# Joining LayerNorm statistics on GpSimd instead of VectorE, with the stages of the pipeline moved to other slots

## The reference, cut to what matters

```python
def _layernorm(x, axis=-1, eps=1e-05):
    m = jnp.mean(x, axis=axis, keepdims=True)
    v = jnp.var(x, axis=axis, keepdims=True)
    return (x - m) / jnp.sqrt(v + eps)
...
h = _layernorm(x, axis=-1) * (1 + ca) + sa
x = x + ga * attn(h)        # attn normalises h again: xn = layernorm(h) * gamma + beta, then q, k, v, rope
h = _layernorm(x, axis=-1) * (1 + cb) + sb
x = x + gb * ffn(h)
```

## Time and profile before

| | us |
|---|---|
| median of three runs (3055.15 to 3060.04) | 3057.6 |
| the profiled execution | 3057.38 |
| its span, first to last instruction | 3055.6 |
| busy: TensorE / VectorE / ScalarE / GpSimd | 2754.5 / 2146.6 / 1816.3 / 967.6 |

### The profile page before, as it was taken

The page is one execution under the profiler, slowest core; times in us unless marked ns, Lnnn a source line. Parts: engine busy times, 40 slices in busy tenths (PEclk is TensorE's granted clock), DMA queues, the critical chain, the costliest instruction groups (busy, mean ns, idle before and its releaser), DMA issues. The chain is left out here.

```text
span 3055.6 us, 48203 instructions
## 1 busy us (share of the span) xinstructions
PE 2754.5 (90%) x17467; PEld 1341.3 (44%) x17467; DVE 2146.6 (70%) x3164; ACT 1816.3 (59%) x3723; POOL 967.6 (32%) x1294
## 2 busy tenths in 40 slices
PE   2788889499999999999999999999999699948997
PEld 0444455134444444444444444444444277734664
DVE  4999999587777777777777777777777155552221
ACT  1667777157777777777777777777777544411121
POOL 1666665311221121122112112211211176732231
PEclk8899999589999999999999999999999899978998
DMA  3367766915444544544554454355443287752342
GB/s 95 123 221 235 216 219 219 203 40 106 95 90 99 103 90 91 106 92 90 102 102 87 94 106 92 86 105 102 86 96 79 69 284 265 266 172 77 91 116 43
DMA packets 188549, 386.18 MB, mean 126 GB/s; under 512 B 33413, under 2 KB 104485, under 8 KB 175800
## 3 DMA queue, kind: packets, MB, share of 16 engines
q1 hardware_dynamic: 182170, 374.58, 47.9%
q0 software_dynamic: 6144, 8.52, 1.6%
HBM read 240.65 MB, written 144.53 MB: 126 GB/s over the span
## 5 line engine op out<-in xcount | busy, mean ns | idle before, releaser
L927 DVE TENSOR_REDUCE mx<-ps 128x2 f32<-128x1024 f32 (+3 forms) x1216 | 1371.4, 1167 | 397.7 <-PE ps L1015 302.3
L973 ACT ACTIVATE prob<-ps 128x512 f32<-128x512 f32 (+1 forms) x2560 | 1251.3, 561 | 539.9 <-PE ps L1033 530.9
L1008 PE MATMUL ps<-k_rows,q_rows 96*128 96x512 bf16 (+3 forms) x3072 | 911.2, 332 | 41.3 <-DMA k_rows<-k_parts 34.6
L1033 PE MATMUL ps<-q_rows,k_rows 99*128 99x512 bf16 (+3 forms) x3072 | 907.0, 328 | 14.6 <-ACT prob L973 6.1
L866 POOL TENSOR_SCALAR_AFFINE_SELECT prob<-prob 128x512 f32<-128x512 f32 x512 | 318.7, 634 | 1452.6 <-ACT prob L973 1452.6
L1052 PE MATMUL ps<-prob,v_rows 128*32 128x512 f32 (+3 forms) x6144 | 628.3, 496 | 0.0
L1033 PEld LDWEIGHTS ps<-q_rows,k_rows 99*128 99x128 bf16 x3072 | 273.0, 98 | 599.1 <-ACT prob L973 360.1
L1008 PEld LDWEIGHTS ps<-k_rows,q_rows 96*128 96x128 bf16 x3072 | 289.9, 98 | 271.6 <-DVE mx L927 60.6
L1015 PE MATMUL ps<-mask_b,unit_b 128*128 128x128 bf16 (+2 forms) x1408 | 348.7, 248 | 0.0
L671 PE MATMUL ps<-x_t,w_all 128*128 128x512 f32 x512 | 250.9, 636 | 0.0
L1052 PEld LDWEIGHTS ps<-prob,v_rows 128*32 128x32 f32 x6144 | 134.3, 108 | 245.9 <-ACT prob L973 122.9
(11 more groups left out here) (154 smaller groups left out, 2683.9 us busy)
## 6 DMA issues: line engine op xcount, KB each, us to landing
k_rows<-k_parts SPq DMA_DIRECT2D x384, 128.0 KB, 7.4
v_ones<-v_st SPq DMA_DIRECT2D x64, 512.0 KB, 4.3
v_rows<-v_ones SPq DMA_DIRECT2D x64, 512.0 KB, 9.3
att<-o_sb SPq DMA_DIRECT2D x128, 256.0 KB, 2.5
att_b<-att SPq DMA_DIRECT2D x16, 2048.0 KB, 9.9
q_parts<-stage SPq DMA_DIRECT2D x128, 192.0 KB, 3.3
k_parts<-stage SPq DMA_DIRECT2D x128, 192.0 KB, 3.3
q_rows<-q_parts SPq DMA_DIRECT2D x64, 384.0 KB, 4.6
```

Source lines behind the costliest of these rows:

```text
L927: dve.tensor_reduce(dst, src, AX.X, ALU.max).then_inc(a_free, 1)
L973: nc.scalar.activation(prob[:, (g * NPC + i) % RING, h, 0:w], src, ACT.Exp).then_inc(exp_done, 1)
L1008: ins = pe.matmul(ps[:, at, col:col + w], q[0:ROWS, g, h, i * P:(i + 1) * P], k[0:ROWS, g, h, k0:k0 + w], start=(r == 0), stop=True, skip_ ...
L1033: ins = pe.matmul(ps[:, PS_B + bank(g, n), at:at + w], k[0:AUG, g, h, j * P:(j + 1) * P], q[0:AUG, g, h, q0:q0 + w], start=True, stop=True)
```

## The change

GpSimd now joins the halves, for eight tiles at once, with seven small instructions per statistic on 128 x 8 elements (`join`: sum and difference of the two means, sum of the two squared deviations, and a chain of four more; ScalarE's root scales by 1/256 and VectorE only takes the reciprocal), and forms the centring term with one more (`centre`). The steps get new leads: take_x 23 -> 27, join_x on GpSimd 23, root 19 -> 22, invert_x 18 -> 21, centre_x 20, first_norm 17 -> 19, modulate 16 -> 18, take_h 15 -> 17, join_h on GpSimd 9, root of h 7 -> 8, invert_h 6 -> 7, centre_h 6; START goes from -23 to -27. In a GpSimd slot join and centre stand ahead of modulate and low. SyncE's program, the three buffers of `xin`, and the slots of everything from second_norm on stay as they are. `link` makes GpSimd wait for its own last instruction before the next.

```diff
@@ -343,8 +343,10 @@
         h = sb("h", [P, 2, T, D], F32)
         stx = sb("stx", [P, T, 6], F32)
         sth = sb("sth", [P, T, 6], F32)
-        agx = sb("agx", [P, 2, T, 2], F32)
-        agh = sb("agh", [P, 2, T, 2], F32)
+        sums = sb("sums", [P, 2, T], F32)
+        gap = sb("gap", [P, 2, T], F32)
+        spread = sb("spread", [P, 2, T], F32)
+        half_sum = sb("half_sum", [P, 2, T], F32)
         rsh = sb("rsh", [P, 2, T], F32)
         nmh = sb("nmh", [P, 2, T], F32)
         sd = sb("sd", [P, 2, T], F32)
@@ -359,6 +361,7 @@
         mod_in = tuple(sem(f"p1_mod_in{r}") for r in range(RING))
         stx_done, sth_done = sem("p1_stx"), sem("p1_sth")
         agx_done, agh_done = sem("p1_agx"), sem("p1_agh")
+        pool_chain = sem("p1_pool_chain")
         sdx_done, sdh_done = sem("p1_sdx"), sem("p1_sdh")
         rsx_done, rsh_done = sem("p1_rsx"), sem("p1_rsh")
         ones_set = sem("p1_ones_set")
@@ -385,7 +388,7 @@
         def turned(n):
             return ps[:, PS_QK + n % QR * 2:PS_QK + n % QR * 2 + 2, :]
 
-        START = -23
+        START = -27
         END = B * T + 6
 
         def batch_at(s, lead):
@@ -450,18 +453,9 @@
                     ins = dve.bn_stats(stx[:, t, :], xin[:, r, t, :])
                 ins.then_inc(stx_done, 1)
 
-            def join_x(b):
-                dve.wait_ge(stx_done, 4 * b + 4)
-                for t in range(T):
-                    ins = dve.bn_aggr(agx[:, b % 2, t, :], stx[:, t, :])
-                ins.then_inc(agx_done, 1)
-
             def invert_x(b):
                 dve.wait_ge(sdx_done, b + 1)
                 dve.reciprocal(rsx[:, b, :], sd[:, 0, :]).then_inc(rsx_done, 1)
-                dve.wait_ge(rsx_done, b + 1)
-                dve.scalar_tensor_tensor(nmx[:, b, :], agx[:, b % 2, :, 0], -1.0, rsx[:, b, :], ALU.mult, ALU.mult) \
-                   .then_inc(statx, 1)
 
             def take_h(b, t):
                 if t == 0:
@@ -474,19 +468,10 @@
                     dve.wait_ge(h_done, (b - 1) * T + t + 1)
                 dve.bn_stats(sth[:, t, :], h[:, b % 2, t, :]).then_inc(sth_done, 1)
 
-            def join_h(b):
-                dve.wait_ge(sth_done, b * T + T)
-                for t in range(T):
-                    ins = dve.bn_aggr(agh[:, b % 2, t, :], sth[:, t, :])
-                ins.then_inc(agh_done, 1)
-
             def invert_h(b):
-                p = b % 2
                 dve.wait_ge(sdh_done, b + 1)
-                dve.reciprocal(rsh[:, p, :], sd[:, 1, :]).then_inc(rsh_done, 1)
-                dve.wait_ge(rsh_done, b + 1)
-                dve.scalar_tensor_tensor(nmh[:, p, :], agh[:, p, :, 0], -1.0, rsh[:, p, :], ALU.mult, ALU.mult) \
-                   .then_inc(stath, 1)
+                reuse(dve, xn_done, (b - 1) * T)
+                dve.reciprocal(rsh[:, b % 2, :], sd[:, 1, :]).then_inc(rsh_done, 1)
 
             def multiply(n):
 
@@ -523,22 +508,18 @@
                     take_rest(n - 1)
                 if s % 2 == 0 and 0 <= n < B * NP:
                     combine(n)
-                b, k = batch_at(s, 18)
+                b, k = batch_at(s, 21)
                 if b is not None and k == 0:
                     invert_x(b)
-                b, k = batch_at(s, 6)
+                b, k = batch_at(s, 7)
                 if b is not None and k == 0:
                     invert_h(b)
-                b, k = batch_at(s, 15)
+                b, k = batch_at(s, 17)
                 if b is not None:
                     take_h(b, k)
-                    if k == T - 1:
-                        join_h(b)
-                b, k = batch_at(s, 23)
+                b, k = batch_at(s, 27)
                 if b is not None and k < 4:
                     take_x(b, k)
-                    if k == 3:
-                        join_x(b)
 
             dve.memset(eps[:, :], EPS)
             for s in range(START, END):
@@ -546,10 +527,10 @@
 
         @block.scalar
         def _(act):
-            def root(b, which, ag, ready, done):
+            def root(b, which, ready, done):
                 reuse(act, rsh_done if which else rsx_done, b)
                 act.wait_ge(ready, b + 1)
-                nc.scalar.activation(sd[:, which, :], ag[:, b % 2, :, 1], ACT.Sqrt, bias=eps[:, :]).then_inc(done, 1)
+                nc.scalar.activation(sd[:, which, :], spread[:, which, :], ACT.Sqrt, bias=eps[:, :], scale=1.0 / D).then_inc(done, 1)
 
             def first_norm(b, t):
                 if t == 0:
@@ -593,12 +574,12 @@
                 nc.scalar.copy(parts(n, 1), rest[:, n % 2]).then_inc(mid_done, 1)
 
             def slot(s):
-                b, k = batch_at(s, 19)
+                b, k = batch_at(s, 22)
                 if b is not None and k == 0:
-                    root(b, 0, agx, agx_done, sdx_done)
-                b, k = batch_at(s, 7)
+                    root(b, 0, agx_done, sdx_done)
+                b, k = batch_at(s, 8)
                 if b is not None and k == 0:
-                    root(b, 1, agh, agh_done, sdh_done)
+                    root(b, 1, agh_done, sdh_done)
                 for tiles, b in turned_in(s - 1):
                     for t in tiles:
                         copy_x(b, t, tiles[-1])
@@ -611,7 +592,7 @@
                 n = (s - 5) // 2
                 if s % 2 == 1 and 0 <= n < B * NP:
                     middle(n)
-                b, k = batch_at(s, 17)
+                b, k = batch_at(s, 19)
                 if b is not None:
                     first_norm(b, k)
                 for tiles, b in normed_in(s):
@@ -635,12 +616,49 @@
                     pool.wait_ge(h_mul, b * T + t + 1)
                     pool.tensor_tensor(h[:, p, t, :], h[:, p, t, :], mods[:, r, M_SA, :], ALU.add).then_inc(h_done, 1)
 
+            links = [0]
+
+            def link(ins):
+                links[0] += 1
+                ins.then_inc(pool_chain, 1)
+                pool.wait_ge(pool_chain, links[0])
+
+            def join(b, which, st, ready, count, rooted, done):
+
+                pool.wait_ge(ready, count)
+                reuse(pool, rooted, b)
+                pool.tensor_tensor(sums[:, which, :], st[:, :, 1], st[:, :, 4], ALU.add)
+                pool.tensor_tensor(gap[:, which, :], st[:, :, 1], st[:, :, 4], ALU.subtract)
+                link(pool.tensor_tensor(spread[:, which, :], st[:, :, 2], st[:, :, 5], ALU.add))
+                link(pool.tensor_scalar(half_sum[:, which, :], gap[:, which, :], D / 4.0, None, ALU.mult))
+                link(pool.tensor_tensor(gap[:, which, :], gap[:, which, :], half_sum[:, which, :], ALU.mult))
+                link(pool.tensor_scalar(half_sum[:, which, :], sums[:, which, :], -0.5, None, ALU.mult))
+                pool.tensor_tensor(spread[:, which, :], spread[:, which, :], gap[:, which, :], ALU.add).then_inc(done, 1)
+
+            def centre(which, nm, rs):
+                return pool.tensor_tensor(nm, half_sum[:, which, :], rs, ALU.mult)
+
             def low(n):
                 pool.wait_ge(mid_done, n + 1)
                 pool.tensor_tensor(parts(n, 2), rest[:, n % 2], parts(n, 1), ALU.subtract).then_inc(lo_done, 1)
 
             def slot(s):
-                b, k = batch_at(s, 16)
+                b, k = batch_at(s, 23)
+                if b is not None and k == 0:
+                    join(b, 0, stx, stx_done, 4 * b + 4, sdx_done, agx_done)
+                b, k = batch_at(s, 9)
+                if b is not None and k == 0:
+                    join(b, 1, sth, sth_done, b * T + T, sdh_done, agh_done)
+                b, k = batch_at(s, 20)
+                if b is not None and k == 0:
+                    pool.wait_ge(rsx_done, b + 1)
+                    centre(0, nmx[:, b, :], rsx[:, b, :]).then_inc(statx, 1)
+                b, k = batch_at(s, 6)
+                if b is not None and k == 0:
+                    pool.wait_ge(rsh_done, b + 1)
+                    reuse(pool, xn_done, (b - 1) * T)
+                    centre(1, nmh[:, b % 2, :], rsh[:, b % 2, :]).then_inc(stath, 1)
+                b, k = batch_at(s, 18)
                 if b is not None:
                     modulate(b, k)
                 n = (s - 6) // 2
```

## The result

The changed kernel takes 3139.6 us in the median of four runs (3135.95 to 3140.32), against 3056.9 for the kernel before on the same chip: a ratio of 1.0267 (95% interval 1.0249 to 1.0285), so 83 us slower. The profiled execution took 3140.32.

What follows compares the result with a forecast made beforehand. Phase 1 was taken to run at VectorE's pace, 29.2 us per batch, becoming a 37.3 us ring behind a late load: 3057.4 + 10.7 + 81 - 8.3 = 3140.8, 3141 us; range 3108 to 3185.

Steps and rivals of the forecast that it cites:

- the late load: Phase 1: take_x comes four slots earlier, its load does not; VectorE waits eleven times, 9 to 13 us each.
- the ring: Phase 1: VectorE statistics, GpSimd work, SyncE k stores and load landing in sequence set a 37.3 us period, 8.1 longer.
- start: Before the first multiply: GpSimd's three joins and two centrings, 6.9 us, partly hidden by an earlier wait; taken as +5.
- first wait ends: Slot 13, load 5: VectorE's take_x waits until 156.0 us instead of standing at 145.35, +10.7.
- ten periods: Phase 1 from load 5 to load 15: ten times 8.1 us longer, +81.
- from the last wait to the end of phase 1: After slot 93 no load is outstanding, so work removed from VectorE counts in full, -8.3 us.
- first rival: Load of x in phase 1 isn't late, so only VectorE's relief counts: faster, 3002 us; chance 0.05.
- The ends of the range: Phase 1: small instructions at 0.14 us, faster landing and issues give period 36.1, about 3125; at 0.5 us some 3180.
- The small instructions: GpSimd's 128 x 8 instructions in phase 1: 0.3 us each with the wait, a join 2.1, a centring 0.3.
- The rule of the Trainium skill: Shared SBUF port of GpSimd and VectorE: moved work might gain nothing, near 3156 us; the forecast kept the full gain.
- Half late: Phase 1: idle ScalarE and GpSimd make low parts sooner, SyncE limits; period 31 us, near 3080; chance 0.07.
- Dear small instructions: GpSimd's small instructions in phase 1 at 0.73 us, a join 5.1; period 45 us, near 3260; chance 0.08.

Runs made afterwards that it cites:

- e1: The changed kernel with load b + 5 of x issued ahead of store b instead of behind it; 3007.61 us, ratio 0.9835 to the kernel before.
- e2: The kernel before with only the lead of take_x and join_x moved from 23 to 27 and START to -27, joins on VectorE; 3137.4 us, ratio 1.0259.
- e5: The changed kernel with each join on GpSimd done twice; 3185.41 us, ratio 1.0419.
- e4: The kernel before with load b + 5 of x issued ahead of store b; 3058.05 us, ratio 1.0000.
- e7: The kernel before with only the two centring products moved to GpSimd, joins, leads, START and loads unchanged; 3041.19 us, ratio 0.9946.

## Why the prediction was right

The forecast was 3141 us, and its mechanism, the late load and the ring, is what the runs show. That the sum is right to 1.4 us is in part luck: the table has errors of up to 2.2 us of either sign, which cancel. Where each step stands in the trace:

The first multiply, the reader of slot 13 with the statistics just before it, the reader of slot 93, and the end of phase 1 on GpSimd:

```profile
...
106.75 1.41 DVE L484 SCALAR_TENSOR_TENSOR m<-ps,bcol,cos_t 128x512 f32<-128x512 f32 x2 [0.43 <-PE ps L689]
...
```

```profile
...
145.87 0.42 DVE L469 BATCH_NORM_STATS2 sth<-h 128x6 f32<-128x256 f32 x1
157.38 0.75 DVE L453 BATCH_NORM_STATS2 stx<-xin 128x6 f32<-128x256 f32 x2 [11.10 <-DMA xin<-in_L_attn_x]
...
```

```profile
...
528.64 0.75 DVE L453 BATCH_NORM_STATS2 stx<-xin 128x6 f32<-128x256 f32 x2 [12.08 <-DMA xin<-in_L_attn_x]
...
```

```profile
...
629.10 4.20 POOL L643 TENSOR_TENSOR stage<-rest,stage 128x1024 bf16<-128x1024 f32 x2 [3.03 <-ACT stage L574]
```

| step | predicted | measured |
|---|---|---|
| start, first multiply against 99.54 (part of the next row) | +5 | 106.75: +7.2 |
| first wait ends | 156.0, +10.7 | 157.38, +12.0 |
| period of the ring | 37.3 us | 371.26 / 10 = 37.1 us |
| ten periods (528.64 - 157.38, before 292.4) | +81 | +78.8 |
| from the last wait to the end of phase 1 (633.3 - 528.6, before 113.5) | -8.3 | -8.9 |
| later phases | 0 | +1.0 |
| sum on the span | +83.4 | +82.9 |

- *VectorE alone would need 25.4 us per batch.* e1 shows 25.3, and 3007.6 against the 3002 of the first rival: its price was right, its condition was not met in the changed kernel.
- *The ring.* VectorE's part was 10.8, measured 11.0 (305.86 to 316.84, the end of the last statistics). From there to the first k store I had 12.9 + 0.4 through the second low part (slot 68 in the prediction, slot 52 in the rows above); measured 13.2, but by another way. The first k store (330.01) does not wait for that low part, which ends at 327.03 + 2.14 = 329.2, but for the issue of the q stores before it, 324.00 + 5.90 = 329.9. In seven of the eleven batches the two ends lie within 0.1 us of each other, and nowhere more than 1.2 apart. That the sum held although the prediction left the q issues out of the ring is luck. The k stores took 5.8 (5.5), the landing 7.4 (7.7).
- *The ends of the range.* They don't come out of the ring as written. With 0.14 us for each of its nine small instructions, a landing of 7.3 and issues of 5.2 the period is 35.2 us and not 36.1. The upper end puts two joins on the ring, 2.8 us more, where the ring holds one join and two centrings, 1.8. The measured time is far from both.
- *The small instructions.* Taken at 0.3 us with the wait; measured 0.20 to 0.23 each, and a whole join 1.72 us (316.92 to 318.64) against 2.1. Two of the groups by line and shape on GpSimd, 200 to 500 us:

```profile
...
L633 POOL TENSOR_SCALAR half_sum<-gap 128x8 f32<-128x8 f32 x16 | 3.7, 231 | 1.4
...
L639 POOL TENSOR_TENSOR nmx<-half_sum,rsx 128x8 f32<-128x8 f32 x8 | 1.6, 202 | 0.0
```

- *The start* was 2 us dearer than taken; the three joins and two centrings named there stand in GpSimd's order as described. The reader's new lead alone is not the cause: in e2 the first multiply starts at 99.85, 0.3 us later than before. With each join done twice (e5) it starts at 114.72, 8.0 us later than in the changed kernel, so the joins are most of it.
- *The rule of the Trainium skill* (page Perfetto Trace Analysis, section Optimizing Scalar/DVE Operations) that moving work between VectorE and GpSimd might not help: in the changed kernel it doesn't help, 3139.6 against 3137.4 of e2, but because of the load. With the load in time it brings 50 us (e1 against e4), and VectorE's remaining instructions, which read at most one operand from SBUF, don't stretch beside a GpSimd that is 91% busy. In e1, 200 to 460 us, the first half of rope has a mean of 728 ns, before 732, and the statistics of h have no idle time and a mean of 397 ns:

```profile
...
L484 DVE SCALAR_TENSOR_TENSOR m<-ps,bcol,cos_t 128x512 f32<-128x512 f32 x86 | 59.5, 728 | 0.4
...
L469 DVE BATCH_NORM_STATS2 sth<-h 128x6 f32<-128x256 f32 x80 | 31.8, 397 | 0.0
...
```

- *Half late*, the second rival, asked that GpSimd run ahead. It does not: it waits 12.10 us for the statistics of h, in the row at 309.35. Its other half came true in part: behind the first low part SyncE issues the q and the k stores with no gap. *Dear small instructions*, the third, fell with 0.2 us.

What the whole change consists of, then: two parts of opposite sign. The joins and centrings on GpSimd, with their new slots, are worth 50 us once the load is in time (e1 against e4); the reader of x four slots earlier costs 79 us by itself (e2); and while the load is late the first is worth nothing.

## What to carry to other kernels

When a step is moved earlier in a software pipeline, its operands must be moved too: follow its load back through the queue that issues it, and write down which slot the transfer in front of it waits for. Compare that slot with the reader's new one; here they were one slot apart, with 5.8 us for the issue of the eight k stores and 7.4 us of landing between them, and issuing the load ahead of store(b) in SyncE's program was the cure. When a long instruction is taken away, look for what it covered: in e7 half of the gain went to a wait that had been hidden behind it. An engine that idles in such a ring is no spare room, and work given to it makes the ring longer.

## What the runs showed of the hardware that was not expected

- The price of a small VectorE instruction with two SBUF inputs depends on what GpSimd does at that moment: 1.66 us beside a low part, with which it ends, and 0.17 us beside an idle GpSimd, for the same 128 x 8 elements. Two of them cost VectorE 2.48 us per batch before, the sixteen joins 1.28.
- A GpSimd instruction on 128 x 8 elements lasts 0.20 to 0.23 us, a bit under a third of one on 128 x 256 (0.73).
- SyncE needs about 0.7 us to issue one store (eight in 5.8 us). Of the sixteen q and k stores ahead of a load, eight stood between the low part of the batch's last piece and that load.
- TensorE's granted clock was 0.50 (1.2 GHz) from 311 to 314 us in e7, after the engine had stood idle for 3.44 us, and eight matmuls took 5.15 us there, 3.60 one projection later. In e1, where TensorE's longest wait for ScalarE's copies from 150 to 480 us is 0.9 us, it was 1.00 from 300 to 400 us.
